# Absolute sums of w_proj by groups of four pieces, a new order of the prologue, and the last four down blocks tile by tile

## The reference

```
x = x + softmax(ln(x)Wq' (ln(ctx)Wk')^T * E^-0.5) (ln(ctx)Wv') Wo + bo
scale = clip(mean(|w|, axis=1), 1e-5);  tern = clip(round(w / scale), -1, 1)
h = ln(x) @ (tern_fc * scale_fc).T + gate * (x @ v.T @ fast_b.T @ u.T)
x = x + (relu(h)^2) @ (tern_proj * scale_proj).T
```

## Time and profile before

| | |
|---|---|
| median of 3 runs | 828.8 us (828.24 to 829.31) |
| profiled execution | 828.39 us, span 826.6 us |
| TensorE matmul busy | 810.5 us (98%), 4185 instructions |
| TensorE weight load busy | 676.5 us (82%) |
| VectorE busy | 514.1 us (62%), 1051 instructions |
| ScalarE busy | 374.5 us (45%), 712 instructions |
| GpSimd busy | 154.1 us (19%), 175 instructions |
| DMA | 36.74 MB, mean 44 GB/s |

### The profile page before, as it was taken

How to read it: one execution, slowest core, us unless ns; L and a number is a source line. 1 busy time by engine, 2 the same in 40 slices (tenths; PEclk the granted TensorE clock), 3 DMA queues, 4 the chain that set the end, 5 groups by cost and what they waited for, 6 DMA issues and landing times.

```text
span 826.6 us, 11140 instructions
## 1 busy us (share of the span) xinstructions
PE 810.5 (98%) x4185; PEld 676.5 (82%) x4185; DVE 514.1 (62%) x1051; ACT 374.5 (45%) x712; POOL 154.1 (19%) x175
## 2 busy tenths in 40 slices
PE   6999999999999999999999999999999999999997
PEld 4678788888888888888888888888888888888886
DVE  5998763676547664676547764586536764477434
ACT  5997463424533263424634254424634255423332
POOL 2250230025001240024100150023300250013001
PEclk9999999999999999999999999999999999999999
DMA  9752010101101011101101011101101010000001
GB/s 317 254 148 91 1 52 1 38 1 52 52 1 39 5 48 50 39 1 51 52 1 40 1 52 51 39 1 52 52 1 39 0 52 1 1 2 26 25 1 51
DMA packets 17485, 36.74 MB, mean 44 GB/s; under 512 B 4596, under 2 KB 4998, under 8 KB 17432
## 3 DMA queue, kind: packets, MB, share of 16 engines
q1 hardware_dynamic: 16868, 34.98, 12.3%
q10 hardware_dynamic: 564, 1.06, 0.3%
HBM read 27.64 MB, written 8.39 MB: 44 GB/s over the span
## 4 chain that ended last, share of the span: by engine, by line
PE 94%; DVE 2%; DMA 2%; SPq 1%; issue 0%; ACT 0%; DVEq 0%
PE H L1194 28%; PE O L1174 28%; PE G L1090 24%; PE G L1118 4%; PE H L1200 4%; DMA Wv_s<-in_L_xattn_Wv_dram 2%; PE H L1074 1%; PE H L1090 1%; PE G L1147 1%; PE H L1118 1%; PE O L1247 1%; PE H L1067 1%; PE O L1215 1%; SPq L461 0%; PE H L1059 0%
## 5 line engine op out<-in xcount | busy, mean ns | idle before, releaser
L1194 PE MATMUL H<-xnT,fcT 128*128 128x512 f32 x1024 | 257.3, 393 | 0.0
L1174 PE MATMUL O<-projT,qbuf 128*128 128x512 f32 x1000 | 250.9, 393 | 0.0
L1194 PEld LDWEIGHTS H<-xnT,fcT 128*128 128x128 f32 x1024 | 188.3, 188 | 36.8
L1174 PEld LDWEIGHTS O<-projT,qbuf 128*128 128x128 f32 x1000 | 184.7, 188 | 37.1 <-DVE qbuf L986 0.3
L718 ACT ACTIVATE qbuf<-rbuf 128x512 fp32r<-128x512 f32 x126 | 79.5, 631 | 125.4 <-PE O L1174 63.6
L986 DVE TENSOR_TENSOR qbuf<-rbuf,qbuf 128x512 fp32r<-128x512 f32 x126 | 94.0, 746 | 65.2 <-ACT qbuf L718 65.2
L982 DVE TENSOR_TENSOR rbuf<-rbuf 128x512 f32<-128x512 f32 x128 | 98.7, 771 | 52.2 <-ACT rbuf L710 51.1
L710 ACT ACTIVATE rbuf<-H,scf 128x512 f32<-128x512 f32 x128 | 87.3, 682 | 81.8 <-PE H L1200 81.6
L571 POOL TENSOR_TENSOR xrs<-xrs,mhalf 128x4 f32<-128x4 f32 x9 | 9.5, 1050 | 347.5 <-DVE xrs L966 347.5
L1090 PE MATMUL G<-n1T,M 128*128 128x512 f32 x276 | 64.2, 390 | 0.0
L1090 PE MATMUL G<-Wvo,tT 128*128 128x512 f32 x270 | 63.9, 389 | 0.2 <-DVE tT L886 0.2
(11 more groups left out here) (169 smaller groups left out, 991.4 us busy)
## 6 DMA issues: line engine op xcount, KB each, us to landing
xb<-in_x_dram SPq DMA_DIRECT2D x8, 1024.0 KB
ctxb<-in_ctx_dram SPq DMA_DIRECT2D x8, 768.0 KB
wring<-in_L_ffn_w_fc_dram SPq DMA_DIRECT2D x16, 256.0 KB, 6.4
wring<-in_L_ffn_w_proj_dram SPq DMA_DIRECT2D x16, 256.0 KB, 3.8
out_dram<-x2a SPq DMA_DIRECT2D x8, 512.0 KB, 2.6
out_dram<-x2b SPq DMA_DIRECT2D x6, 512.0 KB, 2.6
Wq_s<-in_L_xattn_Wq_dram SPq DMA_DIRECT2D x4, 256.0 KB, 4.2
x2a<-in_L_xattn_Wo_dram ACTq DMA_DIRECT2D x1, 1024.0 KB, 11.3
```

Source lines behind the costliest of these rows:

```text
L1174: mm = pe.matmul(banks[f"O{t}"][:, :], qbuf[:, j % 2, h, t * P:(t + 1) * P], projT[:, j, :], start=(j == 0 and h == HI), stop=(j == NFF - ...
L1194: pe.matmul(banks[f"H{j % 2}"][:, :], fcT[:, k, j * P:(j + 1) * P], xnT[:, h, k, :], start=(k == 0 and h == HI), stop=False)
```

## The change

Four things are edited together. First, for w_proj (pieces 16 to 31) the four `abs` of a group become one `sum:g`: a single ACTIVATE over the four pieces of a ring half (2,048 columns), which waits for all four loads, with its elementwise result in the tile nrm; `scale:4` to `scale:7` then need no partial sums. Pieces of w_fc keep their `abs`. Second, all lists of the prologue are laid out anew: the order of the loads, of TensorE's jobs and turns, of ScalarE's and VectorE's work; the joined pieces are other ones (eight in place of nine), store:3 goes to VectorE and wqT:1 to ScalarE. Third, FIRST_LATE is one block earlier: body 7 runs up 13, 14 and 15 in a row and then down 11, and the last four downs (12 to 15) run tile by tile; the late squares lie in n2T in place of pT. Fourth, the last tile's product with the row scales is made in two halves, each followed by the add of its half. Two further words (`lean`, `sign`) are defined, but no list uses them; they are left out of the diff here, with the semaphore `signs_made` that only they use.

```diff
--- before.py
+++ after.py
@@ -41,9 +41,7 @@
 TOK = TILES * P
 NFF = 16
 PIECES = 2 * NFF
-FIRST_LATE = NFF - 2
-LAST_DOWNS = ([(t, j) for t in (0, 1) for j in (NFF - 3, NFF - 2)] + [(0, NFF - 1), (1, NFF - 1)]
-              + [(t, j) for t in (2, 3) for j in (NFF - 3, NFF - 2, NFF - 1)])
+FIRST_LATE = NFF - 3
 ATTENTION = ([("n1T", t) for t in range(4)] + [("n2T", t) for t in range(4)]
@@ -159,46 +157,47 @@
         out += placed(engine, 2 * j + 1) if attention else []
         out += [("lo", j)]
     if not attention:
-        out += [("up", NFF - 2), ("sq", NFF - 2), ("hi", NFF - 2), ("lo", NFF - 2), ("up", NFF - 1), ("down", NFF - 4),
-                ("sq", NFF - 1), ("hi", NFF - 1), ("lo", NFF - 1)]
+        for j in (NFF - 3, NFF - 2):
+            out += [("up", j), ("sq", j), ("hi", j), ("lo", j)]
+        out += [("up", NFF - 1), ("down", NFF - 5), ("sq", NFF - 1), ("hi", NFF - 1), ("lo", NFF - 1)]
     return out
 PROLOGUE = {
     "sp": (
-        "Wq:1 Wq:0 ring:0 ring:1 ring:2 ring:3 Wq:2 Wq:3 ring:4 Wk:1 Wk:0 g2row bqrow Wk:2 x:0 ring:5 ctx:0 ring:6 ring:7 "
-        "Wv:0 ring:8 ring:9 ring:10 ring:11 ring:12 ring:13 ring:14 ring:15 ring:16 bo ring:17 ring:18 ring:19 "
-        "ring:20 lowrank ring:21 ring:22 ring:23 ring:24 ring:25 ring:26 ring:27 ring:28 ring:29 ring:30 ring:31 next "
+        "ring:0 ring:1 ring:2 Wq:0 ring:3 Wq:1 Wq:3 Wq:2 Wk:0 bqrow ring:4 Wk:2 g2row Wk:1 x:0 ring:5 ring:6 ring:7 "
+        "ring:8 Wv:0 ctx:0 ring:9 ring:10 ring:11 ring:12 ring:13 ring:14 ring:15 ring:16 ring:17 ring:18 ring:19 "
+        "ring:20 bo lowrank ring:21 ring:22 ring:23 ring:24 ring:25 ring:26 ring:27 ring:28 ring:29 ring:30 ring:31 "
+        "next "
     ).split(),
     "pe": (
-        "wqT:0 wqT:1 vecs wqT:2 wqT:3 bq:0 turn:0 wkT:0 turn:1 wkT:1 wkT:2 turn:2 M:0 M:1 turn:3 wvT:0 wvT:1 n1T:0 "
-        "n1T:1 M:2 turn:4 turn:5 bv:0 turn:6 turn:7 wvT:2 n1T:2 wvo:0 turn:8 turn:9 n1T:3 turn:10 turn:11 wvo:1 wvo:2 "
-        "turn:12 turn:13 turn:14 n2T:0 turn:15 co:0 M:3 n2T:1 turn:16 fb:0 n2T:2 n2T:3 turn:17 turn:18 turn:19 t:0 "
-        "t:1 t:2 turn:20 turn:21 ut:0 turn:22 s:0 s:1 s:2 pT:0 s:3 ut:1 turn:23 ut:2 turn:24 pT:1 ut:3 w:0 w:1 w:2 "
-        "turn:25 turn:26 turn:27 a:0 a:1 a:2 a:3 turn:28 turn:29 turn:30 turn:31 B.x:0 B.x:1 B.x:2 B.x:3 sprow B.L:0 "
+        "wqT:0 vecs wqT:1 wqT:2 wqT:3 bq:0 wkT:0 turn:0 turn:1 wkT:1 wkT:2 M:0 M:1 wvT:0 turn:2 n1T:0 turn:3 turn:4 "
+        "wvT:1 M:2 turn:5 n1T:1 turn:6 bv:0 wvo:0 wvT:2 turn:7 turn:8 turn:9 turn:10 n1T:2 n1T:3 turn:11 wvo:1 wvo:2 "
+        "n2T:0 n2T:1 turn:12 turn:13 turn:14 turn:15 co:0 fb:0 M:3 turn:16 n2T:2 n2T:3 turn:17 turn:18 turn:19 t:0 "
+        "t:1 t:2 turn:20 turn:21 ut:0 turn:22 s:0 s:1 s:2 ut:1 turn:23 pT:0 s:3 ut:2 turn:24 ut:3 pT:1 w:0 w:1 w:2 "
+        "turn:25 turn:26 turn:27 a:0 a:1 a:2 a:3 turn:28 turn:29 turn:30 B.x:0 B.x:1 B.x:2 B.x:3 turn:31 sprow B.L:0 "
         "B.up:0 B.up:1 B.up:2 "
     ).split(),
     "act": (
-        "abs:0 abs:1 vecs abs:2 abs:3 wqT:0 wqT:2 wqT:3 store:0 abs:4 store:1 store:2 tb abs:5 Wo M:0 abs:6 abs:7 M:1 "
-        "nx0 nx1 wvT:0 wvT:1 abs:8 nx2 abs:9 abs:10 n1T:0 n1T:1 store:3 M:2 abs:11 abs:12 store:4 abs:13 abs:14 "
-        "abs:15 store:5 nc0 wvT:2 nx3 store:6 store:7 n1T:2 n1T:3 wvo:0 nc1 abs:16 abs:17 store:8 store:9 abs:18 "
-        "abs:19 abs:20 store:10 store:11 wvo:1 wvo:2 store:12 nc2 abs:21 abs:22 n2T:0 abs:23 store:13 store:14 "
-        "store:15 n2T:1 nc3 M:3 fb:0 n2T:2 n2T:3 abs:24 abs:25 store:16 store:17 abs:26 abs:27 store:18 store:19 uhi "
-        "t:0 t:1 t:2 store:20 abs:28 n2:0 ut:0 store:21 n2:1 s:0 s:1 n2:2 s:2 pT:0 abs:29 n2:3 ut:1 s:3 store:22 pT:1 "
-        "ut:2 store:23 abs:30 abs:31 ut:3 w:0 w:1 w:2 store:24 store:25 store:26 store:27 store:28 store:29 diag "
-        "B.x:0 B.x:1 B.x:2 B.x:3 B.L:0 sprow_out B.up:0 B.hi:0 B.up:1 store:30 store:31 B.hi:1 "
+        "abs:0 abs:1 abs:2 vecs wqT:0 abs:3 wqT:1 wqT:2 wqT:3 store:0 abs:4 store:1 tb abs:5 M:0 abs:6 abs:7 nx0 "
+        "abs:8 M:1 wvT:0 store:2 Wo abs:9 nx1 abs:10 wvT:1 M:2 n1T:0 n1T:1 abs:11 abs:12 nx2 store:4 store:5 abs:13 "
+        "nx3 abs:14 abs:15 store:6 wvo:0 wvT:2 store:7 store:8 store:9 nc0 nc1 n1T:2 n1T:3 store:10 store:11 sum:4 "
+        "wvo:1 wvo:2 n2T:0 nc2 nc3 store:12 store:13 sum:5 store:14 n2T:1 fb:0 M:3 store:15 n2T:2 n2T:3 sum:6 t:0 uhi "
+        "store:16 store:17 store:18 store:19 t:1 t:2 store:20 n2:0 n2:1 n2:2 ut:0 store:21 store:22 s:0 s:1 n2:3 s:2 "
+        "pT:0 ut:1 ut:2 s:3 pT:1 store:23 store:24 sum:7 ut:3 w:0 w:1 w:2 store:25 store:26 diag store:27 store:28 "
+        "store:29 store:30 B.x:0 B.x:1 B.x:2 B.x:3 sprow_out B.L:0 store:31 B.up:0 B.hi:0 B.up:1 B.hi:1 "
     ).split(),
     "dve": (
-        "wqT:1 bqacc sides:0 sides:1 sides:2 bq:0 wkT:0 wkT:1 wkT:2 xs01 xs23 cs01 sides:3 M:0 M:1 sides:4 tern:5 "
-        "sides:6 tern:7 cs23 n1T:0 n1T:1 M:2 bv:0 tern:8 tern:9 tern:10 sides:11 sides:12 tern:13 wvo:0 sides:14 "
-        "tern:15 coacc n1T:2 n1T:3 wvo:1 wvo:2 tern:16 sides:17 sides:18 co:0 sides:19 n2T:0 n2T:1 M:3 n2T:2 n2T:3 "
-        "uprep fb:0 tern:20 sides:21 sides:22 sides:23 ulo t:0 t:1 t:2 sides:24 sides:25 n2:0 s:0 s:1 s:2 sides:26 "
-        "n2:1 pT:0 s:3 n2:2 n2:3 sides:27 pT:1 B.xs01 B.xs23 sides:28 w:0 w:1 w:2 sides:29 sides:30 sides:31 a:0 a:1 "
-        "nX0 a:2 a:3 nX1 B.nX2 B.nX3 B.x:0 B.x:1 B.x:2 B.x:3 B.cs01 B.L:0 B.sq:0 B.cs23 B.lo:0 B.sq:1 B.lo:1 "
+        "bqacc sides:0 sides:1 bq:0 wkT:0 wkT:1 wkT:2 xs01 xs23 M:0 sides:2 sides:3 sides:4 M:1 sides:5 tern:6 cs01 "
+        "tern:7 cs23 M:2 n1T:0 n1T:1 store:3 bv:0 sides:8 tern:9 sides:10 sides:11 wvo:0 tern:12 tern:13 tern:14 "
+        "sides:15 n1T:2 n1T:3 coacc wvo:1 wvo:2 sides:16 co:0 sides:17 sides:18 sides:19 n2T:0 n2T:1 fb:0 M:3 n2T:2 "
+        "n2T:3 uprep sides:20 sides:21 tern:22 tern:23 ulo t:0 t:1 t:2 sides:24 sides:25 n2:0 s:0 s:1 s:2 sides:26 "
+        "n2:1 pT:0 s:3 sides:27 n2:2 n2:3 pT:1 B.xs01 B.xs23 sides:28 w:0 w:1 w:2 sides:29 sides:30 sides:31 a:0 a:1 "
+        "nX0 a:2 a:3 nX1 B.nX2 B.nX3 B.x:0 B.x:1 B.x:2 B.x:3 B.L:0 B.cs01 B.sq:0 B.cs23 B.lo:0 B.sq:1 B.lo:1 "
     ).split(),
     "pool": (
-        "scale:0 tb xs23 scale:1 cs23 scale:2 scale:3 scale:4 scale:5 residual:0 residual:1 scale:6 residual:2 "
-        "residual:3 scale:7 a:0 a:1 B.xs23 a:2 a:3 B.cs23 "
+        "scale:0 tb xs23 scale:1 cs23 scale:2 scale:3 scale:4 scale:5 residual:0 residual:1 residual:2 residual:3 "
+        "scale:6 scale:7 a:0 a:1 B.xs23 a:2 a:3 B.cs23 "
     ).split(),
 }
@@ -308,6 +307,7 @@
         x2a = sb("x2a", [P, TILES, D])
         bqrow = crow[:, :]
         absj = sprow[:, :].bitcast(BF16).rearrange("p (a d) -> p a d", a=2)
+        absrow = nrm[:, :, :].rearrange("p a d -> p (a d)").bitcast(BF16)
         ybuf = [pbuf[:, 2 * t:2 * t + 2, :].rearrange("p a s -> p (a s)") for t in range(2)] + [
             nrm[:, t, :] for t in range(2)]
@@ -446,7 +446,7 @@
         def squares(b, j):
             if b == NG - 1 and j >= FIRST_LATE:
-                return pT[:, j - FIRST_LATE, :, :, :].rearrange("p h q s -> p h (q s)")
+                return n2T[:, :, j - FIRST_LATE, :]
             return qbuf[:, j % 2, :, :]
         def piece_bank(j):
@@ -592,9 +592,7 @@
                             plink(nc.gpsimd.tensor_scalar(sc, asum[:, j, :], 1.0 / D, EPS, ALU.mult, ALU.max))
                         else:
                             sc, n = spc[:, j - 4:j - 3], 1
-                            plink(nc.gpsimd.tensor_tensor(psum4[:, 0:2], asum[:, j, 0:2], asum[:, j, 2:4], ALU.add))
-                            plink(nc.gpsimd.tensor_tensor(psum4[:, 2:3], psum4[:, 0:1], psum4[:, 1:2], ALU.add))
-                            plink(nc.gpsimd.tensor_scalar(sc, psum4[:, 2:3], 1.0 / HID, EPS, ALU.mult, ALU.max))
+                            plink(nc.gpsimd.tensor_scalar(sc, asum[:, j, 0:1], 1.0 / HID, EPS, ALU.mult, ALU.max))
                         nc.gpsimd.tensor_scalar(half[:, j % 2, 0:n], sc, 0.5, None, ALU.mult)
                         nc.gpsimd.tensor_scalar(nhalf[:, j % 2, 0:n], sc, -0.5, None, ALU.mult
                                                 ).then_inc(scales_made, 1)
@@ -758,6 +756,20 @@
                             act.wait_ge(abs_done, j - 1)
                         nc.scalar.activation(absj[:, j % 2, :], wring[:, j // 4 % 2, j % 4, :], ACT.Abs,
                                              accum_out=asum[:, j // 4, j % 4:j % 4 + 1]).then_inc(abs_done, 1)
+                    elif kind == "sum":
+
+                        for i in range(4):
+                            act.wait_ge(ring_in[(4 * j + i) % 8], 16 * (j // 2 + 1))
+                        act.wait_ge(abs_done, 4 * j)
+                        nc.scalar.activation(absrow, wring[:, j % 2, :, :].rearrange("p a d -> p (a d)"), ACT.Abs,
+                                             accum_out=asum[:, j, 0:1]).then_inc(abs_done, 4)
...
                     elif kind == "vecs":
```

(28 more changed lines are left out.)

21 lines of the change are left out of this document (17 added, 4 removed).

## The result

The changed kernel took 830.88 us (median of 8 executions, 829.29 to 833.07), the kernel before 828.54 (8 executions): a ratio of 1.0031, with a 95% interval of 1.0022 to 1.0040. (The ratios here rest on all executions and differ a little from the quotient of the medians.) It is slower by 2.3 us, where 0.5 us less was predicted, and lies above the forecast range of 826.9 to 830.4. The profiled execution took 829.53 us (span 827.7), 1.1 more than that of before, so the profile shows about half of the loss. The other half is in the slower executions, of which there is no profile for this kernel; the experiments come back to it.

The account below looks back on a forecast made before the run. TensorE was taken to set the pace, in the prologue too from 10 us on. Terms +0.15 + 0 + 0.22 - 0.6 + 0.1 - 0.4 = -0.5 us gave a median of 828.3; eight in ten, 826.9 to 830.4.

Parts of the forecast that it names:

- Pieces and sums: Joined pieces nine to eight, sums for abs: 0.22 us more on TensorE; scale:4's need of four landed pieces hidden.
- Softmax to a:0: From turn:12 to a:0, new order around pT:0 and pT:1: 0.6 us gained, a:0 at about 79.9.
- three signs: wvo:0 starting behind 34, a dear product of 256 columns, or TensorE's gaps from 62 to 80 under 0.5 us.
- It absorbs the 0.4 by which TensorE arrives late: The unchanged chain from s:3 to pT's low part hides TensorE's 0.4 us lateness; w:0 at 74.0 to 74.1.
- Start: Up to M:0: the reordered first loads cost 0, or 0.3 us if TensorE's late start is not hidden.
- turn:2: Moved from ahead of M:0 to behind M:1 on TensorE: costs 0.4 us.
- the pieces: Joined pieces fall from nine to eight: four more small matmuls on TensorE, 0.22 us, at most 0.4.
- 0.57 for Wv: TensorE's wait for Wv, 0.57 us, goes because Wv lands 1.4 us earlier.
- the 0.3 that I expected at wvT:1: TensorE waits 0.3 us at wvT:1 for its bank, as M:1 on ScalarE queues behind nx0 and abs:8.
- Wo: Issued later, at about 25.5, landing between 30.8 and 33.0: no wait at wvo:0, 0.8 us as upper bound.
- rival (c): Slower because Wo lands late and holds wvo:0; 4.6 us, 832.9, if it takes 11.3 again; chance 0.18.
- Sum lengths and the end: Each 2,048-column sum takes 1.98 us; the end gains 0.4 behind the last matmul, loses 0.1 at the low square.

Follow-up runs that it names:

- e10: Kernel before with the new end and the four whole-group sums, in the old lists: 828.68 us against 828.06, 1.0011.
- e3: Changed kernel with bo and the seven small low-rank loads issued between ring:15 and ring:16: 829.27 us against 828.24, 1.0011.
- e6: Changed kernel with each whole-group sum replaced by four abs and GpSimd's partial sums: 829.15 us against 827.78, 1.0016.
- e13: Kernel before with the new end and sums for groups 4, 6 and 7 only, group 5 by four abs: 827.64 us against 828.27, 0.9994.
- e5: Changed kernel with the softmax stretch in the old order: 829.80 us against 827.78 for the kernel before, 1.0024.
- e11: Changed kernel with early low-rank loads, old softmax order, Wo behind tb, and turn:2, sides:2, store:2 ahead of M:0: 827.85 us against 828.06, 0.9999.
- e12: As e11, with piece 5 joined in place of two-sided: 827.76 us against 828.06 for the kernel before, 0.9996.
- e2: Changed kernel with n2T:1 moved ahead of sum:5 and store:14 on ScalarE: 830.34 us against 828.24, 1.0022.
- e14: As e10, with n2T:1 and store:13 ahead of sum:5 on ScalarE: 831.36 us against 828.27 for the kernel before, 1.0036.
- e9: Kernel before with the new end and the new softmax order, ScalarE's words left in place apart from ut:2: 829.34 us against 828.06, 1.0018.
- e4: Changed kernel with the first fifteen loads in the old order: 829.85 us against 828.24 for the kernel before, 1.0027.
- e1: Kernel before with the new end alone, old lists and sums: 827.30 us against 828.24, 0.9989.
- e7: Changed kernel with Wo issued behind tb again, as before: 830.57 us against 827.78 for the kernel before, 1.0030.

## Why the prediction was wrong

**The step that failed** is in "Pieces and sums"; a second one, below, is in "Softmax to a:0". I asked what a whole-group sum needs and answered for scale:4 alone: four pieces landed, "hidden, by some 0.7 us". For group 4 that held. For group 5 I did not ask, though its last piece is ring:23 and the lists, old and new, put the seven small loads three ring loads ahead of it (the change adds bo). The sum waited 1.57 us and then stood 1.9 us in front of n2T:1. An abs that waits for the last piece has 0.63 us to go; a sum has 1.91, so where the last piece sets the time a sum costs 1.3 us, and n2T:3 waited 1.07 and 1.33 us in the changed kernel and in e10. In place of my 0 stands +1.3 at t:0. e3 (1.34), e6 (0.98) and the pair e10 and e13 (1.2 in the medians) show it from three sides. I had also given all the relief of the sums to ScalarE's mean and not looked for the one place where the load, and not ScalarE, is last. None of the three signs that I had named for a wrong prediction came (wvo:0 at 31.55, half products at 0.42, 1.98 us of gaps around pT:1 alone); t:0 at 55.59 in place of 54.5 to 54.8, w:0 and a:0 are what miss.

**"It absorbs the 0.4 by which TensorE arrives late"**, with w:0 at 74.0 to 74.1 and a gain of 0.6 up to a:0, is refuted. Every kernel with that chain and a full clock keeps the distance from t:0 to w:0 (19.72 before, 19.72 after, 19.71 in e5, e11 and e12): the maximum, the exponentials and pT hang on TensorE's own scores, so lateness at t:0 goes on to the end in full, and in place of the gain of 0.6 in the sum stands 0. The pT wait of 1.5 was forecast rightly. That it would have a price through the clock was in no term.

**The clock.** The 4 of the 8 executions with the low mean clock lost 2.8 us more than the others, and with them the median is 830.88 in place of 829.66. That the new softmax order makes such executions frequent in the new lists is shown (23 of 58 against 0 of 44), and that in the profiled ones the lower of the two levels, 1.2 GHz, is granted right behind the waits. The Trainium skill, "TensorE: Matmul & The Clock Gate", says in Part 1 that the clock is set by how busy TensorE has been of late, and the trace agrees: it fell behind 0.50 us of work in 2 us (e2), and 0.09 in 2 (e14). It did not fall in the changed kernel's profile behind 0.69 in 2, nor in e9's behind 0.61, and it did in e10's behind 0.67, so what decides between executions stays open. The 1.2 us that the clock adds to the median is therefore read from this split and not shown by an experiment, and it stays open why removing the order in e5 gained only 0.3 of the median against the kernel before (2.02 above it in place of 2.34): with intervals of 0.8 us on each side it fits a share of up to 1 us and one of none.

**Start** held: the head of the lists cost nothing up to M:0 (16.91; e4). **turn:2** and **the pieces** were mis-sized together. turn:2 no longer filled part of M:0's wait, which is 1.03 in place of 0.53, and is 0.44 more work behind it (of which e11, with turn:2 moved back, won only 0.10 up to M:2). The joined pieces I netted, nine to eight, at 0.22. But of the turns that TensorE runs between M:0 and t:0, where it sets the pace, eight were of joined pieces and now six are (6, 7, 9, 12, 13, 14), 0.44 more; pieces 22 and 23, joined instead, shorten only the stretch from t:0 to w:0, whose 19.72 us the softmax chain sets. Without the sum's wait this 0.88 is about paid by the waits of e1 that went, 0.60 for Wv and 0.23 at t:0: e3 takes 37.34 where e1 takes 37.22. The 0.57 for Wv went, and of the 0.3 that I expected at wvT:1 nothing came as long as turn:2 ran ahead of it, and 0.18 in e11 and e12. Joining one piece gave its 0.22 (e11 to e12). **Wo** did not hold TensorE up in the changed kernel's profile (issued at 23.2, 6.2 us to landing, wvo:0 at 31.55), which is what the sum had; I had put the issue at 25.5. But rival (c) was nearer than its chance: in e2 Wo took 10.0 us and cost 1.61, and in e4 8.8 and 0.77. The landing differs by 4 us between kernels whose loads up to there are the same, so a late issue of Wo is a risk in some executions and not a constant. Issuing it early is no cure by itself: in e7 it landed at 27.5, and ScalarE still waited for ring:23, 2.12 us in place of 1.57. The forecast's figure of 11.3 was one draw of a wide spread.

**Sum lengths and the end** held: the four sums take 1.91 to 2.01 us against 1.98, and the end gave 0.35 in the changed kernel's profile and 0.39 in e1 against 0.4 less 0.1; the wait at the low square was too small to see.

**The account.** Between the profiles of e1 and of the changed kernel lie 2.2 us of span (825.5 to 827.7). 1.46 of it is from M:0 to t:0: 1.26 at the waits behind sum:5 (1.07 and 0.19), 0.88 for turn:2 and the two pieces, less the 0.83 of e1's waits, 1.31 in sum. Nothing lies from t:0 to the first `L`, and 0.2 behind it. The remaining 0.55 is up to M:0 (16.36 to 16.91), and no edit explains it: kernels with e1's lists up to there start M:0 as late as 17.72. In the medians a further 1.2 us goes with the low clock, which makes 3.4 where 3.3 was measured; as 0.55 of that is chance and the 1.2 is not confirmed by e5, the close fit is luck. With all of it mended but the sums kept, e12 has e1's distances from M:0 to the first `L` to 0.03 us, and its span. Its median stands 0.3 under the kernel before and e1's 0.9; that 0.6 is inside the two intervals and was not pursued.

## What to carry to other kernels

An instruction that takes over the work of several also takes over the latest of their waits, and then still has all of its work before it: cost it as (last arrival + whole length), for each of its instances, not once. Where it stands in a hand-written queue, moving the next consumer ahead of it only names another victim (e2, e14); order the loads so that the last piece is early, or leave that one instance in parts (e13). And idle time that a softmax chain keeps either way is better left apart (0.32 ahead of pT:0, 1.07 behind pT:1) than gathered around one small job (0.49 and 1.50 around pT:1): with the second, 23 of 58 executions of the new lists had a mean clock under 0.999, with the first 0 of 44.

## What the runs showed of the hardware

One DMA of 1 MB, Wo, took between 6.2 and 11.3 us from issue to landing over the kernels here, and 6.2, 6.7, 7.8, 8.3, 8.8 and 10.0 in the six that issue it late (the changed kernel and e2 to e6). The issue of the first 256 KB load behind the small low-rank loads held SyncE's queue for 1.72 us, and for 1.36 to 1.54 in the kernel before, e3 and e10, where the median is 0.33; but the issue of ring:23, two loads further on, took 1.38 as well. 3,429 of the 4,340 packets between 38 and 50 us are under 512 bytes. For such transfers the Trainium skill, "DMA: Bandwidth & Descriptors", in its table of specifications, says that below 512 B each one costs a read-modify-write; no run here separates that from the plain number of packets. The kernel before has a mean clock under 0.999 in 16 of 117 executions, and in the four groups that ran beside the experiments those are, by the medians, 0.1, 0.6, 0.7 and 1.2 us slower than its others, while the changed kernel's are 2.8 slower at the same mean clock.
